# Expert stage of a two-layer transformer kernel: two buffers for the turned hidden rows, third matrices fetched at another place in the queue, the second expert's low part in three pieces

## The reference, cut to what matters

```
g = jnp.einsum('nd,efd->enf', xf, W_gate)
u = jnp.einsum('nd,efd->enf', xf, W_up)
y = jnp.einsum('enf,edf->end', jax.nn.silu(g) * u, W_down)
for k in range(TOP_K):
    out = out + y[top_idx[:, k], n_ar] * pi[:, k:k + 1]
```

## Time and profile before

| what | us |
|---|---|
| median of 3 runs | 2128.66 (2126.56 to 2130.59) |
| the profiled execution, its own time | 2129.79 |
| its span in the trace | 2127.6 |
| expert stage, about | 721 to 1411 |
| PE busy in the whole span | 1901.3 (89%) |
| DVE busy, ACT busy | 1332.3 (63%), 1387.7 (65%) |

### The profile page before, as it was taken

The page is one execution under the profiler, slowest core; times in us unless marked ns, Lnnn a source line. Parts: engine busy times, 40 slices in busy tenths (PEclk is TensorE's granted clock), DMA queues, the critical chain, the costliest instruction groups (busy, mean ns, idle before and its releaser), DMA issues. The chain is left out here.

```text
span 2127.6 us, 37531 instructions
## 1 busy us (share of the span) xinstructions
PE 1901.3 (89%) x11671; PEld 1079.5 (51%) x11671; DVE 1332.3 (63%) x2221; ACT 1387.7 (65%) x1586; POOL 738.5 (35%) x696
## 2 busy tenths in 40 slices
PE   6989999999946689889999989958899999999998
PEld 5722333333332468778888878847622222222255
DVE  4511135345667756555555555537599999999967
ACT  5689999999923223233333333326699999999934
POOL 2000111111110213222223223111178988988922
PEclk9989999999965699999999999979999999999999
DMA  6744334433110465555555555449846435364012
GB/s 203 237 103 70 46 74 90 90 83 84 44 41 5 176 226 175 189 168 195 169 175 198 170 185 176 156 171 337 275 64 128 74 53 123 57 153 62 11 82 71
DMA packets 133134, 276.07 MB, mean 130 GB/s; under 512 B 18732, under 2 KB 69166, under 8 KB 132104
## 3 DMA queue, kind: packets, MB, share of 16 engines
q1 hardware_dynamic: 124856, 253.89, 42.9%
q0 software_dynamic: 6816, 18.62, 2.9%
q10 hardware_dynamic: 1248, 0.92, 0.2%
HBM read 365.58 MB, written 96.21 MB: 217 GB/s over the span
## 5 line engine op out<-in xcount | busy, mean ns | idle before, releaser
L1326 PE MATMUL psum<-A_qa,A_ka 50*128 50x512 f32 x2048 | 409.3, 468 | 22.8 <-DVE A_qa L1413 6.2
L1326 PEld LDWEIGHTS psum<-A_qa,A_ka 50*128 50x128 f32 x2048 | 176.7, 186 | 471.6 <-DVE A1f_probs L1423 242.4
L2714 PE MATMUL psum<-e_w_high,e_xT 128*128 x1136 | 372.5, 399 | 15.3 <-issue 15.0
L1547 POOL TENSOR_TENSOR A1f_probs<-A1f_probs,A1f_bias 128x512 f32<-128x512 f32 x256 | 327.8, 1293 | 82.4 <-ACT A1f_probs L1378 82.1
L1423 DVE SCALAR_TENSOR_TENSOR A1f_probs<-psum,A1f_bias 128x1024 f32<-128x1024 f32 x256 | 311.6, 1217 | 23.5 <-PE psum L1326 20.3
L1366 ACT ACTIVATE A0f_probs<-psum 128x1024 f32<-128x1024 f32 x256 | 311.9, 1218 | 3.6 <-PE psum L1326 3.5
L1378 ACT ACTIVATE A0f_probs<-psum 128x1024 f32<-128x1024 f32 x256 | 314.0, 1226 | 0.0
L1345 PE MATMUL psum<-A1f_probs,v 128*32 128x512 f32 x2048 | 273.6, 605 | 17.3 <-POOL A1f_probs L1547 16.3
L1370 ACT ACTIVATE A1f_probs<-A1f_probs 128x1024 f32<-128x1024 f32 x256 | 274.2, 1071 | 4.5 <-DVE A1f_probs L1423 3.7
L1345 PE MATMUL psum<-A0f_probs,v 128*32 128x512 f32 x2048 | 274.3, 608 | 0.0
L1378 ACT ACTIVATE A1f_probs<-psum 128x1024 f32<-128x1024 f32 x256 | 264.1, 1032 | 0.0
(11 more groups left out here) (308 smaller groups left out, 2596.9 us busy)
## 6 DMA issues: line engine op xcount, KB each, us to landing
e_w_raw<-in_experts SPq DMA_DIRECT2D x69, 2048.0 KB, 10.3
e_w_raw<-in_experts SPq DMA_DIRECT2D x72, 1024.0 KB, 6.3
hidden<-e_squares SPq DMA_DIRECT2D x69, 512.0 KB
e_turned<-hidden SPq DMA_DIRECT2D x276, 128.0 KB, 2.8
qk_parts<-L_part SPq DMA_DIRECT2D x64, 512.0 KB, 4.4
A_qa<-qk_parts SPq DMA_DIRECT2D x192, 128.0 KB, 4.4
A_ka<-qk_parts SPq DMA_DIRECT2D x192, 128.0 KB, 6.5
om<-results SPq DMA_DIRECT2D x16, 512.0 KB, 7.3
```

The source lines that it names most:

```text
L1326: mm = e.matmul(ps[:, side * HALF:(side + 1) * HALF], self.qk.ka[rows, s, pair, kt * P:(kt + 1) * P].bitcast(FP32R), self.qk.qa[rows, s, p ...
L1547: e.tensor_tensor(fourth, fourth, self.bias_of(*w[1:], slice(self.FOURTH, GH)).rearrange("p h q -> p (h q)"), ALU.mult).then_inc(self.mult ...
L2714: mm = e.matmul(out, left[part].bitcast(FP32R), moving.bitcast(FP32R), start=start and i == 0, stop=stop and i == 2)
```

## The change

`squares` gets a second buffer, so that DVE's transpose of tile j waits for the store of tile j-2 instead of j-1. The down fetches numbered k leave the end of SP's turn k+3 for its turn k+4, between `fetch_up` and `store_squares`. The second expert's low part becomes three instructions of 2048 columns, in DVE's turns 1, 2 and 3. The fetch of the x rows of turn 8 goes to the end of the stage. ACT's code is the same as before.

```diff
 Experts.allocate
-        self.squares, self.turned = sb("e_squares", [P, F]), sb("e_turned", [P, 2, F])
+        self.squares, self.turned = sb("e_squares", [P, 2, F]), sb("e_turned", [P, 2, F])
 Experts.low_value
-            order += [("second", k)] * (k < self.REST) + [("down", k - self.LAG)] * (k > self.LAG)
-            order += [("up", k - 1)] * (k > 1) + [("gate", k)] * (k < self.LAST)
-            order += [("second", k + 1)] * (k + 1 == self.REST)
+            order += [("second", k)] * (k < self.REST) + [("rest", 3)] * (k == 3)
+            order += [("down", k - self.LAG)] * (k > self.LAG) + [("rest", 2)] * (k == 2)
+            order += [("up", k - 1)] * (k > 1) + [("gate", k)] * (k < self.LAST) + [("rest", 1)] * (k == 1)
 Experts.sync
             self.store_squares(e, j)
             self.load_turned(e, j)
             self.fetch_down(e, flags, j)
-            if j == 8:
-                beside(e, (3,))
-        for j in range(self.BY_PE, MOE_TILES):
-            self.fetch_down(e, flags, j)
+        for k in range(self.BY_PE - 4, self.LAST_FETCH + 1):
+            self.fetch_next_down(e, flags, k)
...
-        beside(e, (0, 1, 2))
+        beside(e, (0, 1, 2, 3))
 Experts.fetch_up
         if j == 2:
-            e.wait_ge(self.low_ready, self.low_value("second", self.REST))
+            e.wait_ge(self.low_ready, self.low_value("rest", 2))
             self.fetch(e, 0, FOURTH, part, self.fourth_in)
         if 1 <= j - 1 <= self.LAST_FETCH:
             e.wait_ge(self.high_ready, self.high_value("up", j))
             e.wait_ge(self.low_ready, self.low_value("up", j - 1))
             self.fetch_next(e, flags, j - 1, part, self.weights_in)
+        if j > 4:
+            self.fetch_next_down(e, flags, j - 4)
+
+    def fetch_next_down(self, e, flags, k):
+        e.wait_ge(self.high_ready, self.high_value("down", k + 1))
+        e.wait_ge(self.low_ready, self.low_value("down", k))
+        self.fetch_next(e, flags, k, (DOWN_AT, WIDE), self.second_in)
 Experts.fetch_down
         elif j == 2:
             e.wait_ge(self.high_ready, self.high_value("up", 3))
+            e.wait_ge(self.low_ready, self.low_value("rest", 3))
             self.fetch(e, 0, FOURTH, part, self.fourth_in)
-        elif 1 <= k <= self.LAST_FETCH:
-            e.wait_ge(self.high_ready, self.high_value("down", k + 1))
-            e.wait_ge(self.low_ready, self.low_value("down", k))
-            self.fetch_next(e, flags, k, part, self.second_in)
 Experts.store_squares
-        e.dma_start(self.hidden_dram[j % 2, :, :], self.squares[:, :]).then_inc(self.squares_out, DMA)
+        e.dma_start(self.hidden_dram[j % 2, :, :], self.squares[:, j % 2, :]).then_inc(self.squares_out, DMA)
 Experts.dve, multiply
-                if j == self.BY_PE:
-                    e.wait_ge(self.squares_out, DMA * j)
-                else:
-                    e.wait_ge(self.h_turned, j - self.BY_PE)
+                e.wait_ge(self.squares_out, DMA * (j - 1))
 Experts.dve
-        def low_second(k):
-            with self.if_second(e, k):
-                e.wait_ge(self.high_ready, self.high_value("second", k))
+        def low_second():
+            with self.if_second(e, 1):
+                e.wait_ge(self.high_ready, self.high_value("second", 1))
                 low_of(slice(0, 1), 0, WIDE)
+            e.drain().then_inc(self.low_ready, 1)
+
+        def low_rest(a, b):
+            with self.if_second(e, self.REST):
+                e.wait_ge(self.high_ready, self.high_value("second", self.REST))
+                low_of(slice(0, 1), a, b)
             e.drain().then_inc(self.low_ready, 1)
 Experts.dve, square
-            if j:
-                e.wait_ge(self.squares_out, DMA * j)
-            e.transpose(self.squares[:, :], self.hid[:, :]).then_inc(self.squared, 1)
+            if j >= 2:
+                e.wait_ge(self.squares_out, DMA * (j - 1))
+            e.transpose(self.squares[:, j % 2, :], self.hid[:, :]).then_inc(self.squared, 1)
 Experts.dve, the loop over tiles
-            if 1 <= j < self.REST:
-                low_second(j)
+            if j == 1:
+                low_second()
             if j >= self.LAG:
                 rest_of_hidden(j - self.LAG)
+            if j == 3:
+                low_rest(DOWN_AT, WIDE)
             if j > self.LAG:
                 low_part(j - self.LAG, "down", DOWN_AT, WIDE)
             if j + 1 < MOE_TILES:
                 split_rows(j + 1)
+            if j == 2:
+                low_rest(DC * F, DOWN_AT)
             if j > 1:
                 low_part(j - 1, "up", DC * F, DOWN_AT)
...
-            if j + 1 == self.REST:
-                low_second(self.REST)
+            if j == 1:
+                low_rest(0, DC * F)
 Experts.pe, wait_for_weights
-                    e.wait_ge(self.low_ready, self.low_value("second", j))
+                    e.wait_ge(self.low_ready, self.low_value("second", 1) if j == 1 else self.low_value("rest", 2))
```

More of the change, by code:

```diff
@@ L2435, in fetch_up @@
             self.fetch_next(e, flags, j - 1, part, self.weights_in)
+        if j > 4:
[4 more added lines that the diff above has]
+        self.fetch_next(e, flags, k, (DOWN_AT, WIDE), self.second_in)
     def fetch_down(self, e, flags, j):
-        part, k = (DOWN_AT, WIDE), j - self.LAG
+        part = DOWN_AT, WIDE
         if j == 0:
@@ L2620, in multiply @@
             if j >= self.BY_PE:
-                if j == self.BY_PE:
-                    e.wait_ge(self.squares_out, DMA * j)
-                else:
-                    e.wait_ge(self.h_turned, j - self.BY_PE)
+                e.wait_ge(self.squares_out, DMA * (j - 1))
                 by = {"q": self.Q, "r": self.R}
-                out = self.squares[:, :].rearrange("p (f q r) -> p q f r", **by)
+                out = self.squares[:, j % 2, :].rearrange("p (f q r) -> p q f r", **by)
                 parts = [x.rearrange("p (q f r) -> p q f r", **by) for x in parts]
@@ L2745, in turn_hidden @@
             for f in range(FC):
-                tr = e.transpose(self.HT[:, f * P:(f + 1) * P], self.squares[:, f * P:(f + 1) * P], self.m.ident[:, :])
+                tr = e.transpose(self.HT[:, f * P:(f + 1) * P], self.squares[:, j % 2, f * P:(f + 1) * P], self.m.ident[:, :])
             tr.then_inc(self.h_turned, 1)
```

## The result

The changed kernel takes 2146.68 us (median of 4 runs, 2144.05 to 2149.61) against 2128.15 us: a ratio of 1.0086, 95% interval 1.0069 to 1.0104. That is 18.5 us slower (14.7 to 22.1 by the interval), where 16.7 were forecast; the time forecast was 2145.4 us. The profiled execution took 2145.85 us.

A forecast was written before the change was run, and what follows sets the result against it. The expert stage was taken as bound by PE, standing at each switch for SP's late count. 1.9 + 6 x 2.3 + 1 = 16.7 us on the profiled 2129.8 gives 2146.5, 2145.4 as median; range 2141 to 2150.

The forecast's parts named there:

- What PE waits for: At expert switches PE waits through DVE and ACT for a late count from SP, not for data or DVE's squares.
- 2.3 us a switch: At each switch the empty down fetch comes behind the up fetch, so PE restarts 2.3 us later.
- a gain of up to 0.46 us: In SP's queue the 2 MB fetch could start 0.46 us earlier; taken as nothing at six switches.
- The first switch and the start: PE leaves the start 4.5 us sooner but keeps only 0.46; the first switch costs 1.9 us net.
- The three pieces: At the start, the second expert's split low part lets PE's gate product start 2.5 us earlier.
- some 2.5 us later: At the start, DVE's second piece ends 2.5 us after PE's turn can start at 746.7, near 749.2.
- the 1.23 us of issue ahead of it: At the start, PE's gate product follows the second piece by 1.23 us of issue, near 750.4.
- its 2 us: At the start, the second squares buffer spares ACT's silus a wait and brings PE some 2 us.
- kept 0.46 us: Of the start's 4.5 us only SP's own gain from the traded fetch order survives, 0.46 us.
- The clock: PE's longer stands bring more low clock level after switches; 1 us for all seven.
- Rival 3: DVE's wait for the squares was the chain, so the change is faster: 2124 down to 2100; chance 0.07.

The follow-up runs named there:

- e1: The changed kernel with the down fetches moved back to the end of SP's turn k+3, behind the loads; 2127.36 us, ratio 1.0005 to the kernel before.
- e2: The kernel before with only the down fetches moved to SP's turn k+4, between up fetch and store; 2145.97 us, ratio 1.0093.
- e3: The changed kernel, but with down fetch j-3 issued between store and loads of SP's turn j from turn 4 on; 2092.6 us, ratio 0.984 to the kernel before.
- e5: The kernel before with only the second buffer for the squares and the x fetch at the end; 2131.45 us, ratio 1.0012.
- e4: The kernel before, one squares buffer, no pieces, with down fetch j-3 issued between store and loads from turn 4 on; 2097.96 us, ratio 0.9863.
- e10: The kernel e3 with the store of the squares issued ahead of both fetches; 2092.02 us, ratio 0.9825 to the kernel before.

## Why the prediction was right

*What PE waits for.* Right, and shown by e1, e2, e3 and e5: it is a count that SP gives late, not data, and not DVE's squares.

*2.3 us a switch.* From the start of the loads to the empty down fetch it was 2.27 us on the mean of the seven switches, and is 4.71 now: 2.44 more (2.28 at the last six, as forecast; 3.32 at the first, where SP took 2.83 us to issue the four loads and not 1.80). PE's restart, counted from the silu of tile k+1, moved by 2.86 us on the mean (25.58 to 28.44). The remaining 0.4 us is the start of the loads, which came later by as much (18.04 to 18.46), since the 2 MB were issued 0.5 us later (7.13 to 7.64). That is the step of the prediction that was mis-sized: it saw that the 2 MB could be issued at another time, as a gain of up to 0.46 us, and took it as nothing at six switches; it was a loss. SP's fetch waits for DVE's low part of up, and that ended later by as much (4.86 to 5.40 after the silu of tile k+1). At the third switch, and most of all at the first, ACT's high part of gate and up had been late too; what delays DVE at the others I did not follow further. e2, which has the move alone, shows 0.3 us of it.

*The first switch and the start.* Right in kind, wrong in two sizes and in the place. The three pieces brought 0.8 us at PE's third gate product (752.98 - 730.11 = 22.9 after the first silu, now 747.79 - 725.74 = 22.05), not 2.5. Two steps failed: that the second piece ends "some 2.5 us later" than PE's turn can start, and "with the 1.23 us of issue ahead of it". DVE and PE after the change:

```profile
743.22 2.29 DVE L2630 TENSOR_TENSOR e_w_low<-e_w_raw,e_w_high 128x2048 fp32r<-128x2048 f32 x1 [1.00 <-issue]
```
```profile
742.37 0.41 PE L2747 MATMUL psum<-ident,e_x 128*128 128x128 f32 x2 [1.78 <-DVE e_xT L2607]
747.79 0.79 PE L2723 MATMUL psum<-e_w_high,e_xT 128*128 x1 [5.01 <-issue]
```

The second piece ends at 745.51, 19.8 us after the first silu and not 19.1; DVE idled 1.00 us ahead of it. That is 0.7 us of the miss. PE starts 2.3 us behind it, not 1.23, which is the rest: PE reads two values of the plan (from 745.88 on), and now both reads stand behind that count, where the first had run beside the turn of the rows (at 751.11). The second buffer brought its 2 us. The lead of 3.6 us at tile 5 was then lost as forecast, but at tile 6 already and not at the first switch. There PE waits for tile 3's hidden rows, whose loads SP issued at 777.12:

```profile
784.83 0.38 PE L2723 MATMUL psum<-e_w_high,e_hT 128*128 x1 [3.05 <-DVE e_hT L2616]
```

By tile 11 the two kernels stood level (100.0 and 100.2 us after the first silu). So the first switch cost the full amount, and nothing of the start was kept, where I had kept 0.46 us: by the silu of tile 16 the changed kernel was 3.7 us behind, and not 1.9. In e1, which has the same start, the lead lasted to tile 11 (97.0) and went at the first switch, so where it is lost is not fixed.

*The clock.* 1 us for all was about right. The low level came at more switches than before (PEclk, third from last: 0.51 after the first and the second, where the earlier trace rows had 0.52 and 1.00):

```profile
862.00:869.00 7.00, 3.85 (x18) 3.86 (x19) 4.79 (x5) 2.51 (x3) 0.00 (x0) 0.51 0.30 85
950.80:957.70 6.90, 4.02 (x19) 4.03 (x20) 4.96 (x5) 2.23 (x3) 0.00 (x0) 0.51 0.29 76
```

From silu k to silu k+5 the seven switches cost 57.6 us over 5 x 8.56 each before and 78.2 now, 20.7 more; 7 x 2.86 = 20.0 of that is PE's later restart. So 0.7 us is left for the clock and all else. From PE's restart to the silu a tile on it was 8.22 to 8.38 us at the seven switches before and 8.23 to 8.39 at six of them now; only the fifth, where the granted clock of that stretch was lowest (0.67, elsewhere 0.70 to 0.77), took 8.63. Between the first silu and the last the clock stood at its low level for 41.0 us before and for 61.4 now. The Trainium skill (TensorE: Matmul & The Clock Gate, Terms) would charge half of each low stretch, so by that estimate 10 us more; this case's trace disagrees again. That DVE sets the pace there is argued from one thing: at the first two switches of the kernel before it idles at most 0.33 us at a time in that stretch.

*Rival 3 and the double buffer.* The advice of the Trainium skill to double-buffer (Trainium Kernel Development and Optimization, Best Practices) is borne out at most behind another cure. In e5 the buffer brings nothing, on top of e4 perhaps 0.2%.

In sum the terms were 1.9 + 13.8 + 1 = 16.7. They measured about 0.2 for the start, 20.0 for seven later restarts and 0.7 for the rest, 20.9 in all. So part of the nearness of the number (2145.4 forecast, 2146.68 measured) is luck: in the two profiled executions the stage grew by 4 us more than the sum, and the medians lie 18.5 us apart, with an interval (14.7 to 22.1) that holds 16.7 and 20.9 alike. The forecast's own span of 2141 to 2150 was also wider than its working: with the first switch at +2.3 and the clock at 3 its terms reach 2148.

## What to carry to other kernels

When an engine waits on a transfer, look up which transfer's count it is: here the profile names a weight fetch, and the fetch moved nothing. An instruction that only counts is best issued before its queue blocks on a landing (e3), and moving one "to the next turn" adds everything that the queue does in between (e2). The longest wait in a list need not be the one to remove; the one that ends last is, and removing another changed the list here and not the time (e5). A further piece is left: of the 0.75 us between the empty fetch and ACT's start, 0.64 is ACT's own read and check of a plan value, which stands behind the wait (860.68 to 861.32 at the first switch of the kernel before). Reading it ahead of the wait was not tried.

## What the runs showed of the hardware that I had not expected

A fetch whose condition is false does not wait for the transfers ahead of it in its queue before it counts. In the kernel before, ACT's read of the plan begins at 860.68, just as the issue of the empty fetch ends (860.58 + 0.10). In e3 the empty fetch was issued at 844.07 behind the 2 MB and the store, and ACT started at 851.27, when that store had not landed (the loads that wait for it start at 853.78). In e10 the 2 MB fetch was issued at 846.01 and the empty one at 846.90, and ACT, which waits for the empty one's count, started at 850.91 with no wait of its own:

```profile
850.91 1.92 ACT L2507 ACTIVATE e_w_high<-e_w_raw  x1 [0.40 <-issue]
```

Between 846 and 851 us that queue had moved 1.30 MB of those 2 MB and of the loads behind them:

```profile
q1 hardware_dynamic: 317, 1.30, 77.4%
```

A real transfer behind the 2 MB does wait: at the seven switches the loads that wait for the 512 KB store began 8.8 to 11.2 us after the store's issue in the kernels before and after, and on the median of all tiles 3.2 us after it in the kernel before (tile 6's store was issued at 796.43 and its loads began at 799.83).
